# Two steps of TensorE's slot in the last two attentions, put in the other order

## The reference

```python
# layer 2: 16 heads of 16, keys and values straight from the context
scores = jnp.einsum('bghsd,bgtd->bghst', qh, kh) * scale
probs = jax.nn.softmax(scores, axis=-1)
out = jnp.einsum('bghst,bgtd->bghsd', probs, vh)
...
# layer 3: 16 heads of 16, queries, keys and values projected, causal
scores = jnp.where(causal, scores, jnp.finfo(scores.dtype).min)
attn = jax.nn.softmax(scores, axis=-1)
out = jnp.einsum('bhqk,bhkd->bhqd', attn, vh)
```

## Time and profile before

| what | value |
|---|---|
| median of 3 runs | 891.35 us (889.71 to 891.43) |
| profiled execution, its time | 891.18 us |
| its span, first to last instruction | 889.0 us |
| what lies around the span | 2.2 us |
| PE busy | 831.1 us (93%) |
| DVE busy | 520.1 us (59%) |
| ACT busy | 361.3 us (41%) |
| mean granted TensorE clock | 0.981 |
| share of PE in the chain that ended last | 82% |

### The profile page before, as it was taken

How to read it: one execution, slowest core, us unless ns; L and a number is a source line. 1 busy time by engine, 2 the same in 40 slices (tenths; PEclk the granted TensorE clock), 3 DMA queues, 4 the chain that set the end, 5 groups by cost and what they waited for, 6 DMA issues and landing times.

```text
span 889.0 us, 13511 instructions
## 1 busy us (share of the span) xinstructions
PE 831.1 (93%) x4982; PEld 629.4 (71%) x4982; DVE 520.1 (59%) x1221; ACT 361.3 (41%) x1179; POOL 77.0 (9%) x98
## 2 busy tenths in 40 slices
PE   6799999999999998899988989989999999999983
PEld 3688888888888886676756668766666666666652
DVE  5667657658665544546486532236787574665643
ACT  2111121112111112676655641128786675665730
POOL 0000120000000000000059300000000000000000
PEclk9999999999999999999998999998999999999996
DMA  8960300000020004100000000000000000000000
GB/s 278 378 162 5 79 1 1 1 1 1 1 98 1 1 0 154 28 1 1 1 2 0 1 1 0 0 0 2 1 2 1 1 2 1 1 1 13 2 17 20
DMA packets 16174, 28.01 MB, mean 32 GB/s; under 512 B 3648, under 2 KB 11824, under 8 KB 15856
## 3 DMA queue, kind: packets, MB, share of 16 engines
q1 hardware_dynamic: 16112, 27.19, 9.6%
HBM read 26.13 MB, written 1.05 MB: 31 GB/s over the span
## 4 chain that ended last, share of the span: by engine, by line
PE 82%; DVE 7%; ACT 7%; issue 2%; DMA 0%; POOL 0%; POOLq 0%; SPq 0%; ACTq 0%; DVEq 0%
PE PS L1452 20%; PE PS L1476 10%; PE PS L1706 5%; PE PS L1682 5%; PE PS L1732 5%; PE PS L1656 5%; PE PS L1541 3%; ACT arena L679 3%; PE PS L1646 3%; ACT arena L768 2%; PE PS L1557 2%; PE PS L1585 2%; PE PS L1573 2%; PE PS L1600 2%; PE PS L1794 2%
## 5 line engine op out<-in xcount | busy, mean ns | idle before, releaser
L601 ACT ACTIVATE arena<-PS 128x256 f32<-128x256 f32 (+3 forms) x192 | 102.5, 560 | 107.0 <-PE PS L1706 39.1
L768 ACT ACTIVATE arena<-PS,W_d 128x256 f32<-128x256 f32 (+1 forms) x256 | 111.3, 455 | 5.6 <-DVE W_d L1175 3.5
L1452 PE MATMUL PS<-XT,W_g 128*128 128x256 f32 (+1 forms) x400 | 98.0, 388 | 0.0
L1452 PE MATMUL PS<-XT,W_u 128*128 128x256 f32 (+1 forms) x400 | 96.0, 383 | 0.0
L1476 PE MATMUL PS<-W_d,mlp_tmp 128*128 128x256 f32 (+1 forms) x400 | 94.1, 379 | 0.0
L643 ACT ACTIVATE tanh_g<-PS 128x512 f32<-128x512 f32 x48 | 28.7, 598 | 157.5 <-PE PS L1452 157.5
L1041 DVE TENSOR_TENSOR mlp_tmp<-mlp_tmp,PS 128x512 f32<-128x512 f32 (+1 forms) x52 | 34.7, 667 | 86.3 <-PE PS L1463 86.1
L1452 PEld LDWEIGHTS PS<-XT,W_u 128*128 128x128 f32 (+1 forms) x400 | 76.6, 191 | 11.2
L1452 PEld LDWEIGHTS PS<-XT,W_g 128*128 128x128 f32 (+1 forms) x400 | 74.6, 192 | 10.9 <-issue 1.2
L1476 PEld LDWEIGHTS PS<-W_d,mlp_tmp 128*128 128x128 f32 (+1 forms) x400 | 72.2, 190 | 8.7
L512 POOL TENSOR_TENSOR RS<-MV,eps 128x2 f32<-128x2 f32 x32 | 6.3, 197 | 790.0 <-DVE MV L880 772.8
(11 more groups left out here) (202 smaller groups left out, 1368.6 us busy)
## 6 DMA issues: line engine op xcount, KB each, us to landing
W_d<-in_w_d SPq DMA_DIRECT2D x1, 3072.0 KB, 10.6
arena<-in_wq SPq DMA_DIRECT2D x4, 512.0 KB, 6.1
arena<-in_wo1T SPq DMA_DIRECT2D x4, 512.0 KB, 7.8
W_g<-in_w_g SPq DMA_DIRECT2D x2, 1024.0 KB, 9.1
W_u<-in_w_u SPq DMA_DIRECT2D x2, 1024.0 KB, 11.0
arena<-in_wkq1T SPq DMA_DIRECT2D x4, 384.0 KB, 6.9
mlp_w<-in_w SPq DMA_DIRECT2D x1, 1408.0 KB, 6.3
W_g<-in_w_g SPq DMA_DIRECT2D x1, 1120.0 KB, 12.2
```

The source lines that it names most:

```text
L601: last = act.activation(dst, src, ACT.Copy)
L768: last = act.activation(PL[:, n % 2, k * S:k * S + w], PS[:, bank + x, i * S:i * S + w], ACT.Exp, bias=NML[:, n % 2, k:k + 1], accum_out=D ...
L1452: last = mm(PS[0:m, k, e * S:(e + 1) * S], w[:, d, f0:f0 + m], XT[p][:, d, :], start=d == 0, stop=d == 1)
```

## The change

In each slot PE issues the values of pair n - 1 before the transposition of pair n, no longer after it. Nothing else is changed, on no engine; waits, banks and buffers are the same.

```diff
@@ -1859,10 +1859,10 @@
                     job_turn(r)
                 if p == 6 and r:
                     job_down(r)
+                if n:
+                    late_values(n - 1)
                 if n < ITEMS:
                     late_turned(n)
-                if n:
-                    late_values(n - 1)
                 if p == 1 and r > 1:
                     job_mixed(r - 1)
                 if p == 2 and r:
```

## The result

The changed kernel takes 906.3 us (median of 4 runs, 904.9 to 908.4); before, 891.3 us. The ratio is 1.0166 (95% interval 1.0145 to 1.0187): 1.7% slower, +15.0 us. The forecast was 908, with a range of 897 to 916. The profiled execution took 908.43 us with a span of 906.4, so it is the longest of the four; its span is 17.4 us longer than the one before, and the late phase in it began 0.9 us earlier, so 18.3 us have to be found after that.

What follows compares the result with a forecast made beforehand. PE was taken to bound the kernel, busy 29.77 of 30 us. Terms 5.7 + 1.5 + 3.6 + 2.35 + 1.2 + 2.6 = 17.0 us on 891.2 gave 908 us; 8-in-10 range 897 to 916.

Steps and rivals of the forecast that it cites:

- Point 1: Input's transposition at p = 0 waits longer for ACT's copy of the denominators, behind slot 7's exponentials, six rounds: 5.7 us.
- Point 2: DVE's string at p = 0 and 1, which `job_mixed` on PE waits for, comes later in rounds 2 and 7: 1.5 us.
- the clock: Rival: two longer waits bring the 1.2 GHz level for about 2 us of work each: +4, 912 us; chance 0.05.
- plain slots: Slots without mask cost nothing: PE needs the copies after 0.93 us, and the next scores give 1.06 us of cover.
- Point 3: Queries at p = 2 of rounds 3 to 6 wait for ACT's copy of `job_mixed`, behind slot 1's exponentials: 3.6 us.
- Point 4: Job's transposition at p = 5: context copy 1.0 us in rounds 3 to 6, DVE's norm 1.35 in 1, 2, 7; together 2.35.
- Point 5: Slots 63 and 64, without scores as cover: values 62 and 63 wait for the copies, 0.75 and 0.45, together 1.2 us.
- Point 6: PE going between weight shapes: net 26 more changes, some in places that wait anyway; 20 x 0.13 = 2.6 us.
- idle time before it doesn't help: Step: ACT's lag of 0.89 us comes from the transposition's place in the same slot, not from work piled up.
- rival of a regained lag: ACT regains part of its lag in slots 7 and 1, halving the denominators' and queries' losses: +11, 902 us; chance 0.18.
- Plain slots that wait: Rival: DVE's copy is 0.3 us late, so some 30 slots without mask lose 0.2 each: +6, 914 us; chance 0.17.
- rival of a gain: At p = 0 and 4 ACT gets the values earlier; 9 waits (4.0 us) and 17 shape changes (2.2) go: 885; chance 0.03.

Runs made afterwards that it cites:

- The kernel with the copy on DVE: Changed kernel, with the copy of the turned denominators (p = 7) moved from ACT's list to DVE's, behind its copy of bank 5: 902.0 us, ratio 1.0118.
- the undoing: Changed kernel, but with the old order in the last slot with two steps (n = 63): 904.4 us, ratio 1.0141.
- the quiet: Kernel before, with the new order only in slots p = 2, 3, 5 and 6: 902.3 us, ratio 1.0125.
- the loud half: Kernel before, with the new order only in slots p = 0, 1, 4 and 7: 904.7 us, ratio 1.0152.
- slot 6 with the later norm: Kernel with the new order in slot p = 6 alone, and DVE's norm of the input after next moved to slot 7: 898.1 us, ratio 1.0077.

## Why the prediction was right, point by point

The outcome is the forecast's case: 906.3 against 908, +15.0 against +17. The mechanism held, that the exponentials and what stands behind them come late and are paid for where PE already waited. That the sum came out so near is partly luck, as points 1, 2 and the clock show. Point by point, new waits from the profile of the changed kernel less those of the kernel before:

| point | predicted us | measured us | from |
|---|---|---|---|
| plain slots | 0 | 0 | pitch 3.07; no wait at L1732 but at the end |
| 1, denominators | 5.7 | 5.3 | 7.0 - 1.7 |
| 2, `job_mixed` | 1.5 | 1.5 | 1.9 - 0.4 |
| 3, queries | 3.6 | 2.5 | 2.1 + 0.8 - 0.4 |
| 4, job's transposition | 2.35 | 1.0 | (2.5 - 2.3) + (4.7 - 3.9) |
| 5, end | 1.2 | 1.3 | two waits at L1732 |
| 6, changes of shape | 2.6 | 2.6 | what is left of 18.3; 1.8 shown, see below |
| clock | 0, a rival with 0.05 | 4.1 | half-clocked groups less their usual length |

The clock's 4.1 are 0.64 for one group of scores at 604.52 us (1.77 and not 1.13), 0.83 and 0.80 for the two groups of 1.89 in round 2, and 1.78 for the last `late_output`. This execution is the longest of four; the one of 904.88 us had a mean clock of 0.979 where this one had 0.974. So the 15.0 us between the medians hold less of it, and they come out 2 below the forecast although the clock took its part, since points 3 and 4 were sized too high by 2.4 us together.

**The plain slots.** The estimate of 0.93 us against 1.06 of cover held.

**Point 1.** The sum was right, but by luck. Its main term was ACT's own copy in slot 7, with the full 0.89 in each of six rounds. The kernel with the new order in slot 7 alone has just this term, and its waits grew by 0.90, 0.79, 0.79, 0.79, 0.45 and 0.32 us, 4.0 in all where 5.3 had been set. What made up for it is DVE's path, which I took for a correction of 0.2 in two rounds. It is a path of full size: slot 6 alone, where ACT's copy of slot 7 is not late at all, makes the same wait 6.4 us, and in rounds 2 to 6 it is at least as long as ACT's. Since only the later of the two is paid, they gave 5.3 together. As a forecast of what half of the change costs, the same reasoning missed by 10 us, about half of it by this path and half by the clock. The step "idle time before it doesn't help", on which the choice against the rival of a regained lag rested, held in the changed kernel: all six waits grew, by 0.7 to 1.1 us. The kernel with the copy on DVE shows that what PE waits for is the end of ACT's list.

**Point 2** held in round 2 (1.37 less 0.38, where 1.05 was set). The rest of its total is luck: in round 7, for which 0.5 was set down, no wait shows, and round 3, for which nothing was, gave 0.58.

**Point 3** was sized too high. The queries wait 0.40, 0.83, 0.83 and 0.84 us, in all 2.9, and not 3.6 and the old 0.4. The three in rounds 4 to 6 are near the 0.9 to 1.0 that were set. In round 3, where 0.75 was set, nothing was added to the old 0.44: there PE had just waited 0.58 us for `divide`, so the loss came under point 2.

**Point 4** was sized too high, mostly at the norm: 0.37 us in rounds 1 and 2 and nothing in round 7, where 0.45 had been set three times. For the context 0.2 in all and not 1.0: PE itself comes a little later by the changes of shape, so the wait grows by less than ACT's lag.

**Point 5.** The place held and the size too, by the waits in the trace; the undoing returned 0.7 of it there.

**Point 6.** The rows of the changed kernel show the price itself: 0.32 and not 0.24 behind the mask, 0.87 and not 0.82 for six transpositions. The total of 2.6 is only what is left over, but most of it can be read from the slots. Slot 6 of round 1 runs from one start of scores to the next, in the kernel before and then in the one with slot 6 alone, which has one change of shape more there and no new wait:

```profile
648.75 1.13 PE L1682 MATMUL PS<-W_g,W_u 32*128 32x256 f32 x8
...
652.71 1.13 PE L1682 MATMUL PS<-W_g,W_u 32*128 32x256 f32 x8
```

```profile
651.23 1.13 PE L1682 MATMUL PS<-W_g,W_u 32*128 32x256 f32 x8
...
655.35 1.13 PE L1682 MATMUL PS<-W_g,W_u 32*128 32x256 f32 x8
```

That is 3.96 and 4.12 us, and the difference is 0.15 to 0.16 in each of rounds 1 to 6; where a change was taken away, in slots 2 and 3, a slot is up to 0.20 shorter. So the estimate of 0.13 for each was near, if a little low. The kernel with the old order in its last slot has no group at the lower clock inside the rounds: its slots 1 to 60 hold 12.1 us more than before, 10.3 of them waits, and the 1.8 left are the net of all changes of shape there. The other 0.8 lies behind them and is not taken apart. By the Trainium skill, "TensorEngine Tiling (Array Packing)", Key Properties, a change of tiling mode drains the engine; the trace agrees as far as these 0.08 and 0.05 us and the 0.15 for a slot go.

**Rivals.** Plain slots that wait, no change, and a gain are excluded by the trace and the time. ACT did stop waiting for the values before its copy of bank 6, as the rival of a gain said, and no wait of PE went by it. A regained lag would have halved points 1 and 3; they came to 7.8 of 9.3. The fall of the clock was rated too low: with a chance of 0.05 and +4 us, it took 4.1 in the profiled execution, and some part in most of the other kernels.

## What to carry to other kernels

A step moved back by 1 us on the engine that sets the time costs nothing where it stands, and is paid at the few places where that engine already waits, however shortly, for the last work of another engine's slot: look for those waits first, and take the shift times their number as a first estimate (single waits grew by 0 to 1.1 us here, for a shift of 0.8). Follow the shift down every list that waits for the moved step: two lists may carry it to the same place, where only the later one is paid, and then the costs of two halves add up to more than the whole (6.5 and 12.1 us against 14.2 here, with the lower clock taken out), so an experiment on one half says little about the other. Where such a place exists, moving the copies that are waited for to an engine that is idle by then can be worth more than the order: here two copies gave 0.3%, in the kernel with the old order, and neither order gave a gain that the time shows.

## What the runs showed of the hardware that was not expected

In the profile before, the granted clock stays at the 2.4 GHz level from about 605 us to the tail. In those of the changed kernel and of five others (the quiet and the loud half, slot 6 alone, slot 6 with the later norm, and the one with the copy on DVE), a wait of 0.8 to 1.4 us is followed by two or three groups at the 1.2 GHz level, although PE was busy for 94 to 97% of the 50 us in front. In the changed kernel this is at 660.38 us, after the wait of 1.42. It isn't there after each such wait: slots 6 and 7 (1.43 us) and the old order in the last slot (1.43 us) have waits as long and no such group inside the rounds. In the changed kernel the wait of 1.42 at 696.49 us is followed by a group of values of 1.06 us. And the wait of 0.83 in slot 5 of round 3, behind which the clock falls in the kernel with the later norm, is in the kernel before too, where it doesn't fall. Transpositions slow down with the clock too (1.09 and 1.89 us for eight).

The first groups of the late phase and the last `late_output` fall to either level from one execution to the next, 1.97 or 3.75 us for the latter. That fits the scatter of the kernel before (889.6 to 893.6 us, with a mean clock of 0.981 to 0.974), which makes differences under 1 us hard to show by the time alone. What decides when it falls stays open; no kernel was made to tell.
